# Count store in four pieces, row scaling on POOL, and no idle products in a graph kernel's edge stage

## The reference

```python
e = leaky_relu(alpha_s[src] + alpha_d[dst], 0.2)
m = segment_max(e, dst)                      # per node and head
ex = exp(e - m[dst])
denom = segment_sum(ex, dst)
msg = h[src] * (ex / (denom[dst] + 1e-16))
out = segment_sum(msg, dst) + bias
```

## Time and profile before

| | us |
|---|---|
| median of 3 runs | 3779.69 |
| lowest, highest | 3767.09, 3793.72 |
| profiled execution | 3786.42 |
| its span | 3784.7 |

### The profile page before, as it was taken

One profiled execution on the slowest core, in us unless ns is written; L12 is line 12 of the kernel. 1 busy time (PEld: TensorE's weight loads), 2 busy tenths in 40 slices (PEclk: granted clock), 3 DMA queues, 4 the chain that ended last, 5 costly groups with the idle time before them and its releaser, 6 DMA issues. The chain is left out here.

```text
span 3784.7 us, 70413 instructions
## 1 busy us (share of the span) xinstructions
PE 3206.7 (85%) x17613; PEld 2175.8 (57%) x17614; DVE 2294.0 (61%) x7564; ACT 1514.8 (40%) x3233; POOL 1503.5 (40%) x1510
## 2 busy tenths in 40 slices
PE   2767889888888888867999999999697898988878
PEld 1445656666666666654555555555353666666644
DVE  7566888888788887784232323232442566666668
ACT  3144545444545454434131313131264555555522
POOL 4143444444444443201636363632000266666600
PEclk9878999999899998987999999999799999999989
DMA  3369886788777877823545454544288244444410
GB/s 88 75 217 278 167 168 169 160 169 182 154 163 165 171 171 152 139 58 117 175 131 172 137 171 132 171 137 124 70 199 204 90 125 122 126 124 122 120 50 21
DMA packets 492933, 537.98 MB, mean 142 GB/s; under 512 B 233309, under 2 KB 409131, under 8 KB 492489
## 3 DMA queue, kind: packets, MB, share of 16 engines
q1 hardware_dynamic: 399001, 281.52, 32.5%
q0 software_dynamic: 82592, 237.73, 21.6%
q10 hardware_dynamic: 11280, 18.02, 1.3%
HBM read 414.48 MB, written 102.16 MB: 137 GB/s over the span
## 5 line engine op out<-in xcount | busy, mean ns | idle before, releaser
L1104 POOL DMA_INDIRECT rows<-att_dram,idx x512 | 577.6, 1128 | 793.2 <-PE p_out L1167 563.2
L1167 PE MATMUL p_out<-rows,hot 128*128 128x266 f32 x2048 | 610.2, 424 | 0.4 <-DVE rows L1316 0.4
L1664 PE MATMUL p_lo<-cbuf,parts 128*128 128x400 f16 x1750 | 581.8, 332 | 0.0
L1665 PE MATMUL p_hi<-cbuf,parts 128*128 128x400 f16 x1750 | 581.8, 332 | 0.0
L1735 POOL DMA_INDIRECT rec_dram<-records,edge_place x416 | 409.6, 985 | 409.7 <-PE p_hi L1768 200.7
L2247 POOL DMA_INDIRECT col_rows<-col_dram,m_idx x440 | 416.3, 946 | 254.2 <-issue 140.5
L1167 PEld LDWEIGHTS p_out<-rows,hot 128*128 128x128 f32 x2048 | 381.8, 208 | 49.7 <-DVE rows L1316 0.7
L1692 DVE TENSOR_TENSOR node_sum<-p_hi,low_sb 128x400 f32<-128x400 f32 x80 | 45.9, 574 | 544.0 <-ACT low_sb L1683 544.0
L1316 DVE TENSOR_TENSOR rows<-rows 128x512 f32<-128x512 f32 x512 | 348.4, 681 | 0.2 <-ACT rows L1072 0.2
L1683 ACT ACTIVATE low_sb<-p_lo 128x400 f32<-128x400 f32 x80 | 39.8, 504 | 567.9 <-PE p_hi L1665 563.3
L1665 PEld LDWEIGHTS p_hi<-cbuf,parts 128*128 128x128 f16 x1750 | 171.2, 98 | 131.5 <-issue 9.5
(11 more groups left out here) (462 smaller groups left out, 6291.5 us busy)
## 6 DMA issues: line engine op xcount, KB each, us to landing
cbuf<-count_dram SPq DMA_DIRECT2D x40, 2500.0 KB
count_dram<-x_sb SPq DMA_DIRECT2D x32, 1500.0 KB
dl_rep<-dl_dram SPq DMA_DIRECT2D x128, 256.0 KB
g_rows<-count_dram SPq DMA_DIRECT2D x25, 800.0 KB, 4.7
rec_dram<-blank ACTq DMA_DIRECT2D x1, 17600.0 KB, 74.6
m_group_rows<-rec_dram SPq DMA_DIRECT2D x110, 160.0 KB, 2.2
records<-in_edges POOLq DMA_DIRECT2D x32, 520.0 KB, 4.4
pen<-pen_dram SPq DMA_DIRECT2D x512, 8.0 KB
```

Source lines behind the costliest of these rows:

```text
L1104: nc.gpsimd.indirect_dma_start(rows[r][:, u, :], None, att_dram, bass.IndirectOffsetOnAxis(ap=idx[r][:, u:u + 1].bitcast(U32), axis=0)).th ...
L1167: m = nc.tensor.matmul(p_out[:, side, 0:HALF], hot[k][:, u, :], rows[k][:, u, side * HALF:(side + 1) * HALF], start=(u == 0), stop=(u == U ...
L1664: nc.tensor.matmul(p_lo[m][:], parts[:, k, m, 1, :], cbuf[q][:, k, :], start=(k == 0), stop=(k == NT - 1))
L1665: r = nc.tensor.matmul(p_hi[m][:], parts[:, k, m, 0, :], cbuf[q][:, k, :], start=(k == 0), stop=(k == NT - 1))
```

## The change

Five edits, all in the edge stage.

1. The store of a round is cut in four pieces of 7, 6, 6 and 6 of the 25 node tiles (`PIECE`), one in each step of SP, and of round i - 2 in round i, where it was of round i - 1. A piece is 256 columns wide, not 240. Each piece waits for the one before. `stored` so rises by 64 a round. The last two rounds are stored whole at the end.
2. `scale_sums` moves from DVE to POOL, behind the four gathers of its step, and is done for step j in POOL's step j. `add_sums` waits for it (`scaled`), as does `rescale` on ACT before it overwrites `scale`.
3. Every product of `add_up` counts (`summed`), so each gather waits only for the product that used its chunk of the buffer.
4. Two of the six pairs of one-hots stand in the chain of `zz`, and the place instructions end with round 24: DVE's loop is split in two.
5. `keep_clock` and its bank are gone.

```diff
-PER = 11
+PER = 10
+PIECE = (0, 7, 13, 19, 25)
...
-                            if k == 3 and not is_first(i):
-                                store(i - 1, i)
-
-                        def store(r, i):
-                            sp.wait_ge(evacuated, i * 4)
+                            if not (isinstance(i, int) and i < 2):
+                                store(i - 2, PIECE[k], PIECE[k + 1], i * 64 + (k * 16 - 112))
+
+                        def store(r, first, last, before):
+                            sp.wait_ge(evacuated, r * 4 + 4)
                             sp.nop().then_inc(waits_passed, 1)
-                            sp.wait_ge(stored, i * 16)
+                            sp.wait_ge(stored, before)
...
-                            sp.dma_start(count_dram.rearrange("(k p) n -> p k n", p=P)[:, :, bass.ds(to, WIDE)],
-                                         taken[:, :, bass.ds(side, WIDE)]).then_inc(stored, 16)
+                            sp.dma_start(count_dram.rearrange("(k p) n -> p k n", p=P)[:, first:last, bass.ds(to, AT)],
+                                         taken[:, first:last, bass.ds(side, AT)]).then_inc(stored, 16)
...
-                        store(ROUNDS - 1, ROUNDS)
-                        sp.wait_ge(stored, ROUNDS * 16 + 16)
+                        for r in range(ROUNDS - 2, ROUNDS):
+                            store(r, 0, NT, (ROUNDS - 2) * 64 + (r - ROUNDS + 2) * 16 + 16)
+                        sp.wait_ge(stored, (ROUNDS - 2) * 64 + 48)
...
                         def edge_hot(g, r):
                             if not (isinstance(g, int) and g < 4):
-                                act.wait_ge(sums_ready, g - 3)
+                                act.wait_ge(summed, (g - 3) * U)
...
                         def rescale(g, q):
                             act.wait_ge(fall_ready, g + 1)
+                            if not (isinstance(g, int) and g < 2):
+                                act.wait_ge(scaled, g - 1)
...
                             if r is not None and not is_first(r):
-                                act.wait_ge(stored, r * 16)
+                                act.wait_ge(stored, r * 64 - 48)
...
-                        def work(j, k, i):
+                        def work(j, k, tiles):
                             if within(j, 3):
                                 pool.wait_ge(idx_ready, j + 4)
-                                if not is_first(j):
-                                    pool.wait_ge(sums_ready, j)
+                                for u in range(U):
+                                    if not is_first(j):
+                                        pool.wait_ge(summed, j * U - (U - 1 - u))
+                                    pool.nop().then_inc(waits_passed, 1)
+                                    gather((k + 3) % 4, u)
+                            scale_sums(j, k % 2, tiles[k])
+
+                        def scale_sums(j, q, tile):
+                            pool.wait_ge(scale_ready, j + 1)
+                            pool.nop().then_inc(waits_passed, 1)
+                            if not is_first(j):
+                                pool.wait_ge(added, j)
                                 pool.nop().then_inc(waits_passed, 1)
-                                for u in range(U):
-                                    gather((k + 3) % 4, u)
+                            own = heads(acc[:, bass.ds(tile, 1), 0:SUMS].rearrange("p o s -> p (o s)"))
+                            nc.gpsimd.tensor_tensor(own, own, scale[q][:].unsqueeze(2).broadcast_to([P, HW, HEAD]), ALU.mult).then_inc(scaled, 1)
...
-                            if u == U - 1:
-                                m.then_inc(sums_ready, 1)
+                            m.then_inc(summed, 1)
...
-                            keep_clock(2)
...
                         def add_sums(j, tile):
-                            dve.wait_ge(sums_ready, j + 1)
+                            dve.wait_ge(scaled, j + 1)
+                            dve.wait_ge(summed, j * U + U)
...
                             n = o.did(TT(zz[:], p_tab[:, :, 0:HW], slots(k), ALU.add))
+                            TT(rows[k][:, :, SUMS:], attr4_step[:, bass.ds(j * U, U), :], rows[k][:, :, SUMS:], ALU.mult)
                             o.need(n)
                             n = o.did(STT(zz[:], zz[:], 0.2, zz[:], ALU.mult, ALU.max))
+                            if ahead:
+                                if before:
+                                    dve.wait_ge(counted, j)
+                                count_hots(j + 1, 1 - q, 0, 1)
                             o.need(n)
                             n = o.did(TT(zz[:], zz[:], p_tab[:, :, HW:], ALU.subtract))
-                            TT(rows[k][:, :, SUMS:], attr4_step[:, bass.ds(j * U, U), :], rows[k][:, :, SUMS:], ALU.mult)
+                            if ahead:
+                                count_hots(j + 1, 1 - q, 1, 2)
                             o.need(n)
                             TS(zz[:], zz[:], 0.0, None, ALU.min).then_inc(arg_ready, 1)
-                            n = scale_sums(j - 1, 1 - q, tile_before) if before else o.skip(1)
...
-                            o.did(edge_places(k, i))
+                            if places:
+                                o.did(edge_places(k, i))
...
+                        for first, last, places in ((1, NT, True), (NT, ROUNDS - 1, False)):
```

More of the change, by code:

```diff
@@ L1123, in _ @@
                         nc.gpsimd.memset(x_sb[:], 0.0).then_inc(empty_ready, 1)
-                        rounds(pool, work)
+                        body(0)
+                        with pool.Fori(1, ROUNDS - 1) as i:
+                            body(i)
+                        body(ROUNDS - 1)
                         pool.wait_ge(blank_out, 16)
@@ L1221, in at_word @@
                                                       skip_runtime_bounds_check_because="the word holds at most v places at step v when it is made")
-                        def keep_clock(n):
-                            for i in range(n):
-                                nc.tensor.matmul(idle[:], ident16[:], nothing[:, 0:240], start=True, stop=True, skip_group_check=True)
                         def body(i, last):
@@ L1317, in weigh, with work @@
                                ALU.mult).then_inc(msg_ready, 1)
-                        def scale_sums(j, q, tile):
-                            dve.wait_ge(scale_ready, j + 1)
-                            if not is_first(j):
-                                dve.wait_ge(added, j)
-                            own = heads(flat(acc[:, bass.ds(tile, 1), 0:SUMS]))
-                            return o.did(TT(own, own, over(scale[q][:], HEAD), ALU.mult))
                         def add_sums(j, tile):
-                            dve.wait_ge(sums_ready, j + 1)
+                            dve.wait_ge(scaled, j + 1)
+                            dve.wait_ge(summed, j * U + U)
                             own = flat(acc[:, bass.ds(tile, 1), :]).rearrange("p (s n) -> p s n", s=2)
                             TT(own, own, p_out[:, :, 0:HALF], ALU.add).then_inc(added, 1)
-                        def work(j, k, i, tile_before, tile_after):
+                        def work(j, k, i, tile_before, tile_after, places):
                             o.enter(j)
@@ L1402, in _ @@
                         for k in range(4):
-                            work(k, k, 0, tiles[k], tiles[k + 2])
-                        with dve.Fori(1, GROUPS // 4 - 1) as i:
-                            tiles = read_registers(nc, group_table, i * 4 - 1, 6, ET.DVE, NT - 1)
-                            for k in range(4):
-                                work(i * 4 + k, k, i, tiles[k], tiles[k + 2])
+                            work(k, k, 0, tiles[k], tiles[k + 2], True)
+                        for first, last, places in ((1, NT, True), (NT, ROUNDS - 1, False)):
+                            if not places:
+                                o.leave(first * 4)
+                                o.begin(PER - 1, first * 4)
+                            with dve.Fori(first, last) as i:
+                                tiles = read_registers(nc, group_table, i * 4 - 1, 6, ET.DVE, NT - 1)
+                                for k in range(4):
+                                    work(i * 4 + k, k, i, tiles[k], tiles[k + 2], places)
                         tiles = (*read_registers(nc, group_table, GROUPS - 5, 5, ET.DVE, NT - 1), None)
                         for k in range(4):
-                            work(GROUPS - 4 + k, k, GROUPS // 4 - 1, tiles[k], tiles[k + 2])
+                            work(GROUPS - 4 + k, k, GROUPS // 4 - 1, tiles[k], tiles[k + 2], False)
                         o.need(o.n)
                         tile = tiles[4]
-                        n = scale_sums(GROUPS - 1, 1, tile)
-                        o.need(n)
                         add_sums(GROUPS - 1, tile)
```

41 lines of the change are left out of this document (21 added, 20 removed).

## The result

| | before | changed |
|---|---|---|
| median of 4 runs, us | 3786.70 | 3828.35 |
| lowest, highest | 3767.09, 3799.77 | 3813.08, 3834.56 |
| profiled execution, its span | 3786.42, 3784.7 | 3813.08, 3811.4 |

The ratio is **1.0088** (95% interval 1.0048 to 1.0129). The prediction was 3686 us, range 3610 to 3810; the kernel became slower by about 1%, and the time lies outside. Ratios from two chips that differ by less than a point are not enough to rank two kernels: where the kernel before takes 4090 to 4098 us, the profiles spend 2456 to 2488 us behind the start of the last round, elsewhere 2206 to 2227, and none shows the kernel before there. Round means are given beside them for that reason.

The account below looks back on a forecast made before the run. DVE was taken to bound a clean round, with some 8 us more lost in an ordinary one. 25 x (40.0 - 43.6) + 3 x (40.0 - 36.1) - 15.5 = -94 from 3779.7 gave 3686 us, range 3610 to 3810.

Parts of the forecast that it names:

- (d): Store in four pieces: gather waits go, but the evacuation waits for the last piece; +3.4 us a round, bounds 1.0 and 6.5.
- The landing: Time from the last piece's issue until it lands and the evacuation can start: 4.8 us, between 3.5 and 6.2.
- (a): Row scaling leaves DVE: 0.63 us less, four times a round, -2.5 us a round.
- (c): Scaling on POOL holds DVE's instructions beside it: 0.95 us a step, +3.8 us a round; bounds 0 and 1.4 a step.
- The rival without a hold: POOL's product doesn't hold DVE: clean step 7.85 us, round 38.1, time 3632 us; chance 0.15.
- (b): One-hots inside DVE's score chain fill time between dependent links: about 0.2 us less a step, -0.8 us a round.
- (e): No products on PE's idle bank: 0, as DVE, not PE, is last in a clean step.
- The clock rival: PE's clock falls without the idle products: +5 us in an 8.8 us step, time from 3750 us up; chance 0.04.
- (f): Place work on DVE ends after round 24: 2.2 us a round for 7 rounds, -15.5 us.
- The gathers: Gathers have slack twice, behind smaller pieces and issued up to 5 us earlier, so waits for rows should go.
- the slow piece with the long product: Last piece lands 6.2 us after issue and POOL locks 1.2 us a step: round about 43.0, 3770 us; chance 0.17.
- The held piece: Gathers hold the last piece some 6 us longer: round 46.7, time 3873 us; no gain from 8.2 us landing; chance 0.12.

Follow-up runs that it names:

- e9: The changed kernel with each store piece issued one SP step earlier and the one-hots in their old order; ratio 0.9583 to the kernel before.
- e4: The kernel before with the row scaling on POOL and nothing else changed; ratio 1.0164 to the kernel before.
- e6: The kernel before without the eight products a step on the unused bank, nothing else changed; ratio 0.9981 to the kernel before.
- e3: The changed kernel with the eight products a step on the unused bank put back; ratio 1.0194 to the kernel before.
- e14: The kernel before with its store in three early pieces, none in the step of DVE's loop turn, and no products on the idle bank; ratio 0.9499.
- e12: The changed kernel with pieces one SP step earlier, but scaling on DVE, old one-hot order and one DVE loop; ratio 0.9641 to the kernel before.
- e8: The kernel before with every store's first column rounded down to a multiple of 16, leaving counts in wrong columns; ratio 0.9427.
- e11: The kernel before with its store alone cut in four pieces, each issued one SP step earlier than in the changed kernel; ratio 0.9524.
- e7: The changed kernel with pieces one SP step earlier, row scaling back on DVE and one DVE loop; ratio 0.9632 to the kernel before.
- e2: The changed kernel with the row scaling back on DVE, all else as changed; ratio 1.0032 to the kernel before.

## Why the prediction was wrong

The forecast round was 35.9 us of steps, 0.7 of turn and 3.4 of stall, 40.0. Measured, in the round at 496.47: 8.7, 8.8, 8.8 and 8.7, some 35.0 of steps (8.8 for the second is that of its neighbours), 2.0 of turn and 7.1 of stall, 44.1.

- **(d), the stall, is the step that failed.** Mechanism and place were right, and so were the issue at +7.2 (503.65, 7.18 us into the round) and the place of `absent` without a stall (+11.7; here 11.6). Two terms of its size were not. *The landing:* the evacuation began 6.8 us after the issue in this round, 6.4 in the mean, not 4.8. I took the fast first 2 us of the last store for what a piece gets, and named 6.2 as the other end. That store is not aligned either; its first 0.46 MB ran fast for a reason that I can't show. *The clock:* it stood at 0.7. From the evacuation's end to `absent` it took 3.29 us where the earlier trace rows has 1.86, 1.4 more; and from `absent` on the step took its usual 5.9, so that the 0.95 to be won there, less 0.7, did not come. 3.4 + 2.0 + 1.4 + 0.25 make the 7.1. Rounds 11 and 13, with equal landings, differ by 2.9 us with the clock. The +8.1 at which the evacuation was to stand (it could have begun at +7.3) was wrong too, but is no term of the sum.
- **The turn of the loop stood nowhere.** Its 0.67 us was in the earlier trace rows as "issue"; I kept it as a constant. It is a latency from the end of `falls` on (2.77 us in the kernel before), covered in part by what stands behind; the change took cover away (0.8 us, e9) and put a store there. 1.3 us a round is 37 us.
- **(a) and (c), the scaling.** Predicted -0.63 and +0.95 a step; the hold is 0.66 in the row shown, so the exchange is about even. The rival without a hold fell with the row at 524.14. Where the product falls decides (e4).
- **(b), the one-hots.** -0.8 us a round was right for the steps (e9), and the turn took it back.
- **(e), the idle products.** 0 was right beside the old waits (e6); beside the new one taking them out gained about 1% (1.0088 against 1.0194 in e3; 43.95 against 46.06 us a round). The clock rival was real where no long wait is, and tiny (e14); beside a long turn a low clock cost the step behind it 0.8 to 1.6 us (e12).
- **(f), the place instructions.** -15.5 us was wrong: a step without a wait went from 8.85 to 8.75 us, 0.4 a round. They stood between two dependent links, and my reading, which no run tests, is that this gap stays.
- **The gathers** went as forecast: no waits for rows. Their cause stood in the three clean rounds, which I subtracted and did not explain; it was worth more than the whole change (e8).

Of the rivals, the slow piece with the long product came nearest (round 43, 3770 us), and of it only the slow piece was true. The held piece (landing at 8.2 us) did not come about: 7.7 us was the longest from the fourth round on.

## What to carry to other kernels

When a transfer is cut up and moved nearer to its reader, write down issue, landing and need for the last piece; if they are closer than the slowest landing seen, move the issue a step earlier, which here turned 1.009 into 0.960. Price the clock with the stall: a wait that leaves PE idle was here followed by work at 1.2 GHz, on the path. Before subtracting the rounds that go well, ask what sets them apart; here it was the first byte of a row. The idle time at a loop's turn is a latency that other work covers: what is moved away from there, or a DMA that is put there, shows up in it.

## What the runs showed of the hardware

- Stores of 480-byte rows to DRAM moved 122 GB/s when the rows began off a 32-byte boundary and 250 GB/s when they began on one, at the same busy share of the DMA engines (1.26 and 1.22).
- While such a slow store ran, gathers on another queue came up to 9.5 us late, 174.4 us in all between 400 and 1400 us; with the store aligned (e8) it was 44.4 us there, and with it cut in quarters, issued early and not aligned (e11) 43.4.
- Beside a product on POOL a bf16 one-hot of 0.25 us took 0.91 and a 128x16 difference of 0.16 us took 1.75; both ended with the product.
- Behind a long wait TensorE's work ran at a clock of 0.50: the same products between an evacuation and `absent` took 3.29 us, against 1.82 at 1.00. In e7 the step behind the loop's turn took 10.69 us with 6.8 us at 0.50, and 9.55 with 3.4.
- A turn of DVE's loop, from the end of `falls` to the next `zz`, took 2.77 us in round after round of e8, and up to 4.1 while a piece of a store was under way (e11).
- A loop in whose rounds three to five packets of the instruction queue came took up to 9.1 us a turn in place of 2.0 (e2); that its code was loaded anew is my reading.
